# Masked cross attention with the mask of each key in the same matmul pass as the head's features

## The chip, the cores and the metric

The kernel runs on one core of a Trainium2 chip. The metric is the device time of one launch in microseconds (us). Five engines work in parallel, each through its own instructions in order: TensorE (PE, matmuls), VectorE (DVE), ScalarE (ACT), GpSimd (POOL) and SyncE (SP), which here issues nearly all DMA transfers. They wait for each other through semaphores.

## The reference, cut to what matters

A stream `x` of 4 batches of 512 tokens of 128 features passes four blocks of cross attention, each followed by a feed-forward block. The keys and values come from a context of 77 tokens. The fourth block is a decoder of four layers, each with causal self attention, masked cross attention and a feed-forward part. Masked cross attention is, for each head:

```python
scores = jnp.einsum('bhqd,bhkd->bhqk', q, k) / np.sqrt(DK).astype(jnp.float32)
scores = jnp.where(mask[:, None, :, :] == 0, jnp.float32(-1000000000.0), scores)
p_attn = jax.nn.softmax(scores, axis=-1)
x = jnp.einsum('bhqk,bhkd->bhqd', p_attn, v)
```

There are three masks: `l0` (all ones in these inputs) for block 0, `l1` (a padding mask or a mask by key) for block 1, `l3` (a window over segment numbers) for the four layers of block 3. Heads have 8 features, in block 1 there are 32 heads of 4.

## The kernel before

Cross attention is eight **units** of 16 heads (`UNITS`): 0 (mask `l0`), 1 and 2 (the two halves of block 1, mask `l1`), 3 (block 2, no mask), 4 to 7 (the layers, mask `l3`). A unit runs over 4 batches `b`; the heads lie in 4 groups `g` of 4 heads (`G`, `HG`). A head has 32 rows (`HR`): its features in a high part twice and a low part, and two rows for the negated maximum of each query, so that a product gives exact logits minus the maximum.

For each batch a unit does: normalise and project the queries (`stats`, `apply`, `turn`, `q_project`), project the context to keys and values (`kv_project`, `kv_cut`, `kv_spread`), cut the queries into parts (`q_cut`), transpose them (`q_turn`, into the buffers `q_g`), take scores with queries on the partitions for the maxima (`max`, lines 789 to 805 on PE, line 1311 on DVE), transpose again with the maxima in place (`q_full`), and then `logits` with keys on the partitions: eight tiles per batch, `logits(n, b, g, hp)`, each with two heads side by side. ACT takes the exponential (line 1791), and `values` multiplies by the values. In a masked unit a head's logits are **two** accumulating matmuls over 512 queries: the mask `bias_k` (77 keys, bf16) times the identity, then `kx` (the keys of the group, other heads' rows zero, 128 rows) times `q_g`.

`bias_q` (mask with queries on the partitions) is written by DVE: at the start for `l0`, in `masks1` (lines 1370 to 1381) for `l1`, in `masks3` for `l3`. `mask_turn` transposes it into `bias_k` on PE and ACT. SP's `masks1` (lines 638 to 651) does two things: it clears the tables `slots_in` and `slots_out` in DRAM from a blank row in `f2x`, which POOL zeroes as one of its first instructions, and it loads the raw `l1` masks, as soon as their buffer in `hid` is free.

The order of all work is written out by hand: `program_order` builds a list of steps, `interleaved` runs the phases of up to several batches (prepare, scores, attend, finish) beside each other, row by row, and every engine goes through that one list and does its share of each step. So the attend phase of a batch runs beside the scores phase of the next and the preparation of the one after. `need(...)` makes an engine wait for events, `made(...)` and `landed(...)` give them; `T.slot` and `T.freed` hand out buffers of a ring in order. PSUM has three `wide` buffers of two banks and two `acc` buffers, shared by all steps.

`f2x` holds the scales and the transposed values of the quantised feed-forward block (`quantise`, `turn("f2")`, `f2_matmul`), `f2_hid` its result.

Of the kernel before, what the change touches and what calls it, by code (L numbers as in the profile page):

```python
# [6 lines left out]
P = 128  # L7
# [8 lines left out]
MROW, KROW, QROW = 24, 26, 27  # L16
VSUM = 8
HIGH = -(1 << 12)
NEG = -float(2 ** 100)
E8 = 8  # L20
# [179 lines left out]

CLEARS = 9


def cross_steps(n):
    u = UNITS[n]

    def prepare(b):
# [9 lines left out]
        first = [[("apply", "u", n, b)], [], [], [("turn", "u", n, b)]] if u["first"] else []  # L217
        return s + beside(first, context_steps(n, b)) + query

    def scores(b):  # L220
        s = [[("q_turn", n, b, 0)]]
        for g in range(G):
            for half in range(2):
                s.append([("max", n, b, g, half)] + ([("q_full", n, b, g - 1)] if half and g else [])
                         + ([("q_turn", n, b, 1)] if g == 0 and half else []))
        return s

    def attend(b):
# [5 lines left out]
        tiles[7] += [("values", n, b, 2), ("o_turn", "u", n, b, 0)]  # L234
        return tiles + [[("o_norm", "u", n, b, 0)], [("values", n, b, 3)]]
# [116 lines left out]
def program_order():  # L352
# [17 lines left out]
    for l in range(NL):  # L370
        project, rotate, items = self_steps(l)
        if l == 0:
            items[5][0] = beside(items[5][0], in_rows(*[(3 * k, ("masks3", k)) for k in range(4)]))
            items[6][0] = beside(items[6][0], in_rows((5, ("mask_turn", "l3"))))
# [51 lines left out]
def build(nc, io):  # L426
# [4 lines left out]
    with ExitStack() as ctx:  # L431
# [30 lines left out]
        o_tok = bufs("o_tok", 2, lambda n: sb(f"o_tok{n}", [P, NI, D]))  # L462
        hid = bufs("hid", 2, lambda n: sb(f"hid{n}", [P, 4, S]))
        bias_q_raw = sb("bias_q", [P, NT * SK // 2])
        bias_k_raw = sb("bias_k", [P, B * S // 2])
        bias_q = bias_q_raw[:, :].bitcast(BF).rearrange("p (t k) -> p t k", t=NT)
        bias_k = bias_k_raw[:, :].bitcast(BF).rearrange("p (b s) -> p b s", b=B)
# [18 lines left out]
        f2_hid = bufs("f2_hid", 2, lambda n: sb(f"f2_hid{n}", [P, NI, D]))  # L486
        f2x = bufs("f2x", 2, lambda n: sb(f"f2x{n}", [P, 2 * NI + S // 2]))
# [3 lines left out]

        slots_in, slots_out = (nc.dram_tensor(name, (SLOTS + SPARE, D), F32) for name in ("slots_in", "slots_out"))
# [90 lines left out]
        def sync(e):  # L583
# [54 lines left out]
            def masks1():  # L638
                am_w, pm_w, *_ = raw_masks1()
                blank = f2x[0][:, 0:P]  # L640
# [10 lines left out]
                e.dma_start(pm_w, io["pad_mask"].partition_broadcast(P)).then_inc(*landed("load_masks1", ("masks1",)))  # L651

# [46 lines left out]
            do = dict(unit_end=unit_end, f0_down=f0_down, masks1=masks1, extras=extras, masks3=masks3, slots_in=slots_in_,  # L699
# [12 lines left out]
        def tensor(e):  # L712
# [94 lines left out]
            def logits(n, b, g, hp):  # L807
                masked, tile = UNITS[n]["masked"], ("logits", n, b, g, hp)
                s = wide[T.slot("wide", tile)]
# [1467 lines left out]
```

## Time and profile before

| | us |
|---|---|
| median of 3 runs | 2294.93 (2286.55 to 2299.99) |
| the profiled execution | 2294.56 |
| its span, first to last instruction | 2292.8 |

| engine | busy us | share of the span | instructions |
|---|---|---|---|
| PE | 1955.7 | 85% | 13195 |
| DVE | 1451.5 | 63% | 3533 |
| ACT | 1075.4 | 47% | 1517 |
| POOL | 634.3 | 28% | 865 |

Windows read below: 230.50 to 333.40 is unit 1, 1346.00 to 1372.90 one batch of unit 5, 1465.00 to 1695.20 the self attention of the third layer.

The mean granted TensorE clock is 0.907 of full speed (1.00 is 2.4 GHz, 0.50 is 1.2 GHz). Busy time of PE is modelled: matmuls are pipelined and overlap, so the start times tell more than the durations. PEld is the load of weights, beside PE. "idle before" in a row is the time for which the engine had nothing to do just before, with what released it. Masked logits run at 43 to 132 us (unit 0), 230 to 426 (1 and 2), 950 to 1038, 1320 to 1408, 1695 to 1784 and 2069 to 2158 (4 to 7).

### The profile page before, as it was taken

To read this page: it belongs to the slowest core of one execution; us is meant where nothing else is said; L and a number is where in the kernel's file an instruction comes from. 1 tells how busy PE (TensorE), PEld (TensorE's weight loads), DVE (VectorE), ACT (ScalarE), POOL (GpSimd) and SP (SyncE) were. 2 spreads that over 40 slices of the span, in tenths; PEclk is the share of its full clock that TensorE was granted. 3 is DMA by queue.
4 is the path that set the end of the run, shared out by engine and by line. 5 is a ranking of instruction groups with operands and counts; after the bars stand their busy time and mean duration, and the time that the engine had idled before them with its cause. 6 is when DMAs were issued, how large, how long until landed. Compare 5 with 4: busy or idle time off the path is not lost.

```text
span 2292.8 us, 34000 instructions
## 1 busy us (share of the span) xinstructions
PE 1955.7 (85%) x13195; PEld 1183.1 (52%) x13195; DVE 1451.5 (63%) x3533; ACT 1075.4 (47%) x1517; POOL 634.3 (28%) x865
## 2 busy tenths in 40 slices
PE   5977999585787798999799899898899988989977
PEld 4546666364544344555444565544455544456553
DVE  7545655653777777754666764567675467776468
ACT  2542555221453466553466455356545336545510
POOL 1111000423534353201444210345320144421020
PEclk9988999777786799999899899889889979989988
DMA  7001000121000000000000000000000000000000
GB/s 248 14 1 56 1 1 13 37 84 41 20 1 12 1 1 1 4 7 12 15 1 1 1 10 12 15 1 1 1 4 8 1 14 2 1 1 11 1 1 19
DMA packets 26929, 38.60 MB, mean 17 GB/s; under 512 B 5384, under 2 KB 20112, under 8 KB 26128
## 3 DMA queue, kind: packets, MB, share of 16 engines
q1 hardware_dynamic: 24720, 32.23, 4.3%
q0 software_dynamic: 2048, 4.20, 0.6%
q8 instruction: 104, 1.70, 0.3%
q14 instruction: 57, 0.47, 0.1%
HBM read 25.93 MB, written 10.49 MB: 16 GB/s over the span
## 4 chain that ended last, share of the span: by engine, by line
PE 46%; DVE 12%; ACT 5%; issue 5%; POOL 1%; DMA 0%; DVEq 0%; POOLq 0%; ACTq 0%
PE wide L717 33%; PE acc L717 13%; DVE maxima L1626 4%; ACT prob L1868 2%; DVE hid L1145 1%; DVE x L1687 1%; POOL rstd L1926 1%; DVE hid L1302 1%; ACT prob L1791 1%; DVE qkv L1594 1%; DVE hn L1223 1%; ACT hn L1756 1%; DVE hn L1225 0%; ACT q_g L1712 0%; DVE moments L1178 0%
## 5 line engine op out<-in xcount | busy, mean ns | idle before, releaser
L1626 DVE TENSOR_REDUCE maxima<-wide 128x2 f32<-128x512 f32 (+3 forms) x512 | 407.7, 820 | 182.9 <-PE wide L717 179.3
L1868 ACT ACTIVATE prob<-wide 128x768 f32<-128x768 f32 (+1 forms) x384 | 332.4, 881 | 157.9 <-PE wide L717 156.9
L1791 ACT ACTIVATE prob<-wide 77x1024 f32<-77x1024 f32 x256 | 260.4, 1018 | 148.8 <-PE wide L717 148.8
L717 PE MATMUL wide<-q_g 32*128 32x256 f32 (+3 forms) x2048 | 282.0, 417 | 41.1 <-ACT prob L1868 15.6
L1311 DVE TENSOR_REDUCE maxima<-wide 128x8 f32<-128x616 f32 x256 | 203.0, 796 | 169.4 <-PE wide L717 168.2
L2071 POOL TENSOR_SCALAR_AFFINE_SELECT prob<-prob 128x256 f32<-128x256 f32 (+1 forms) x384 | 185.7, 489 | 387.7 <-ACT prob L1868 383.7
L717 PEld LDWEIGHTS wide<-q_g 32*128 32x128 f32 x2048 | 147.2, 201 | 229.9 <-issue 114.8
L717 PE MATMUL wide<-q_g,kx 128*77 128x512 f32 x512 | 256.0, 572 | 7.7 <-DVE maxima L1311 5.4
L1926 POOL TENSOR_TENSOR rstd<-moments,cst 128x4 f32<-128x4 f32 x88 | 89.7, 1019 | 578.6 <-DVE moments L1199 296.3
L1712 ACT ACTIVATE q_g<-wide 128x1024 fp32r<-128x1024 f32 x128 | 131.2, 1025 | 209.1 <-PE wide L717 209.1
L1712 ACT ACTIVATE q_g<-acc 128x512 fp32r<-128x512 f32 x192 | 114.5, 596 | 186.6 <-PE acc L717 186.1
L717 PE MATMUL wide<-kx,q_g 128*128 128x312 f32 x512 | 181.3, 420 | 7.0 <-DVE maxima L1311 5.0
L717 PE MATMUL wide<-bias_k,ident_b 77*77 77x512 bf16 x448 | 172.4, 385 | 15.0 <-DVE vx L1246 8.7
L717 PE MATMUL acc<-cst,hid 128*128 128x128 f32 x768 | 123.2, 285 | 48.4 <-DVE hid L1302 48.4
L717 PE MATMUL wide<-cst,hid 128*128 128x128 f32 x768 | 122.9, 302 | 34.6 <-POOL A L2061 8.0
L717 PE MATMUL wide<-bias_q,ident_b 128*128 128x312 bf16 x448 | 135.8, 310 | 14.2 <-DVE vx L1246 10.2
L717 PE MATMUL acc<-prob,A 128*32 128x512 f32 (+3 forms) x1408 | 144.3, 486 | 0.0
L717 PE MATMUL acc<-prob,vx 77*32 77x512 f32 x1024 | 138.9, 615 | 0.0
L717 PE MATMUL wide<-causal_b,ident_b 128*128 128x128 bf16 (+1 forms) x768 | 134.4, 261 | 0.0
L717 PEld LDWEIGHTS wide<-cst,hid 128*128 128x128 f32 x768 | 96.0, 155 | 60.8 <-issue 24.2
L717 PE MATMUL wide<-hT,ffn_w 128*128 128x512 f32 x256 | 120.9, 597 | 3.9 <-DVE hid L1636 3.9
L717 PEld LDWEIGHTS acc<-cst,hid 128*128 128x128 f32 x768 | 93.7, 146 | 56.1 <-DVE hid L1302 43.0
(228 smaller groups left out, 3125.2 us busy)
## 6 DMA issues: line engine op xcount, KB each, us to landing
A<-in_w SPq DMA_DIRECT2D x2, 2048.0 KB, 12.4
unit_w<-in_unit_w SPq DMA_DIRECT2D x8, 448.0 KB, 3.4
ffn_w<-in_ffn_w SPq DMA_DIRECT2D x4, 768.0 KB, 4.4
slots_in<-f2x SPq DMA_DIRECT2D x1, 2560.0 KB, 23.6
prob<-slots_in SPq DMA_DIRECT2D x8, 320.0 KB, 3.1
slots_out<-A SPq DMA_DIRECT2D x8, 320.0 KB, 2.2
slots_out<-f2x SPq DMA_DIRECT2D x1, 2048.0 KB, 29.5
unit_w<-in_unit_rows SPq DMA_DIRECT2D x8, 192.0 KB, 4.1
```

Source lines behind the costliest of these rows:

```text
L717: return e.matmul(out, lhsT, rhs, start=start, stop=stop, is_transpose=turn)
L1145: return e.tensor_scalar(out.bitcast(I32), src.bitcast(I32), HIGH, None, ALU.bitwise_and)
L1223: i_op = e.tensor_scalar(dst[:, i, :], src[:, i, :], r[:, i:i + 1], None, ALU.mult)
L1302: return e.tensor_tensor(v[:, :, :, MROW + 1], top, v[:, :, :, MROW], ALU.subtract)
L1311: e.tensor_reduce(maxima[g % 2][:, 2 * half:2 * half + 2, :], v, AX.X, ALU.max, negate=True).then_inc(*made("max", ("free", tile)))
L1594: e.tensor_tensor(qkv[:, 2 * half:2 * half + 2, 0:2 * D], v[:, :, 0:2 * D], bias[:, :, 0:2 * D], ALU.add).then_inc(*made("qkv", ("qkv_adde ...
L1626: e.tensor_reduce(top[:, t, h], v[:, :, at0:at0 + P * t + P], AX.X, ALU.max, negate=True).then_inc(*made("max", *([("free", tile)] if t == ...
L1712: return e.activation(out, src, ACT.Copy, bias=0.0, scale=1.0)
L1791: e.activation(p[0:SC, :], s[0:SC, :], ACT.Exp, bias=0.0, scale=1.0).then_inc(*made("exp", pb, ("free", tile)))
L1868: e.activation(pv, sv, ACT.Exp, bias=0.0, scale=8 ** -0.5).then_inc(*made("exp", pb, ("free", tile)))
L1926: e.tensor_tensor(rstd[T.slot("rstd", held)][:, :], mo[:, 8 * NI:9 * NI], const("minus_half"), ALU.pow).then_inc(*made("rstd", held))
L2071: e.affine_select(out=v, in_=v, compare_op=ALU.is_ge, fill=0.0, base=0, pattern=[[0, many], [1, P]], channel_multiplier=-1).then_inc(*made ...
```

## The change

A masked head's logits become **one** matmul over 32 + 77 = 109 rows (`MASKED`): rows 0 to 31 are the head's own features, rows 32 to 108 one row for each key, with the identity in the keys' operand (`masked_k`) and the mask in the queries' operand (`masked_q`). A head's rows must be brought to partitions 0 to 31 for it, which SP does by DMA.

- New buffers: `masked_q`, three (`AHEAD`) of [128, 2, 512]; `masked_k`, two of [128, 2, 4, 79]; `alive`; `mask_rows`, the turned masks in DRAM. `bias_k` goes. To make room `f2_hid` moves into `A`, the transposed quantised values into one buffer within `bias_q`, and the blank row for the clears into `o_tok[0]`.
- `fetch(n, b, g, hp)` on SP copies two heads' queries from `q_g` into a `masked_q` buffer, 64 KB each, and for the first three tiles of a batch also the 77 mask rows, twice side by side (308 KB), from DRAM. It waits for the buffer (the logits three tiles before), `q_filled` and the mask. `fetch_keys(n, b, half)` copies the keys of 8 heads in 4 transfers. The fetch for tile k + 3 stands in the order behind the logits of tile k.
- `mask_turn` writes the turned mask into `masked_q` buffers; SP stores it to DRAM.
- Queries of which every key is masked are multiplied by zero (`find_alive` on DVE once per mask, a multiply of the projected queries on POOL once per batch of a masked unit); DVE's `q_cut` waits for that.
- POOL zeroes the blank row at its place in `masks1`, and SP's clears, and so its loads of the raw masks behind them, wait for that. `o_norm` of unit 1 waits for the clears. `masks3` and `mask_turn("l3")` stand four items later.

```diff
@@ scores(b), attend(b) in cross_steps
+        if b == 0:
+            for half in range(2):
+                s[4 + 4 * half] += fetch_keys(b, half)
+            for k in range(AHEAD):
+                s[6 + k] += fetch(b, k)
...
+        for k in range(2 * G):
+            tiles[k] += fetch(b + (k + AHEAD) // (2 * G), (k + AHEAD) % (2 * G))
+        tiles[4] += fetch_keys(b + 1, 0)
+        tiles[7] += fetch_keys(b + 1, 1)
@@ sync: masks1
-                blank = f2x[0][:, 0:P]
                 for w in need(("blank_rows",)):
                     e.wait_ge(*w)
                 e.dma_start(slots_in[0:SLOTS, :].rearrange("(p c) d -> p c d", p=P),
...
+            def mask_turn(name):
+                for w in need(("mask_turned", name)):
+                    e.wait_ge(*w)
+                for h in range(2):
+                    e.dma_start(mask_rows[name][:, 2 * h:2 * h + 2, :], masked_q[h][0:SC, :, :].bitcast(F32)).then_inc(
+                        *landed(f"store_mask_{name}", ("mask_k", name)))
+
+            def fetch(n, b, g, hp):
+                tile, name = ("masked_q", n, b, g, hp), UNITS[n]["masked"]
+                at = T.slot("masked_q", tile)
+                to, sem, q = masked_q[at], f"fetch{at}", q_g[T.slot("q_g", ("q_g", n, b, g // 2))][:, g % 2, :]
+                for w in need(T.freed("masked_q", tile), ("q_filled", n, b, g), ("mask_k", name)):
+                    e.wait_ge(*w)
+
+                if 2 * g + hp < AHEAD:
+                    e.dma_start(to[HR:MASKED, :, :].bitcast(F32), mask_rows[name][:, b, :].unsqueeze(1).broadcast_to([SC, 2, S])).then_inc(
+                        *landed(sem))
+                for ii in range(2):
+                    r = HR * (2 * hp + ii)
+                    e.dma_start(to[0:HR, ii, :].bitcast(F32), q[r:r + HR, :].bitcast(F32)).then_inc(*landed(sem, *([tile] if ii else [])))
+
+            def fetch_keys(n, b, half):
+                tile = ("masked_k", n, b, half)
+                at = T.slot("masked_k", tile)
+                for w in need(T.freed("masked_k", tile), ("kv", n, b), ("masked_ones",)):
+                    e.wait_ge(*w)
+                for i in range(HG):
+                    e.dma_start(masked_k[at][0:HR, :, i, :].bitcast(F32),
+                                kx[HR * i:HR * i + HR, i, 2 * half:2 * half + 2, SK * b:SK * b + SK].bitcast(F32)).then_inc(
+                        *landed(f"fetch_keys{at}", *([tile] if i == HG - 1 else [])))
@@ tensor: logits
-                for w in need(T.freed("wide", tile), ("mask_k", masked) if masked else None):
+                for w in need(T.freed("wide", tile), *((held, keys) if masked else (("q_filled", n, b, g),))):
...
                     if masked:
-                        mm(bank, ident_b[0:SC, 0:SC], bias_k[0:SC, b, :], stop=False)
-                    if ii == 0:
-                        for w in need(("q_filled", n, b, g)):
-                            e.wait_ge(*w)
-                    i_mm = mm(bank, kx[:, i, g, SK * b:SK * b + SC], q[:, :], start=not masked)
+                        i_mm = mm(bank, masked_k[T.slot("masked_k", keys)][0:MASKED, g % 2, i, 0:SC],
+                                  masked_q[T.slot("masked_q", held)][0:MASKED, ii, :])
+                    else:
+                        i_mm = mm(bank, kx[:, i, g, SK * b:SK * b + SC], q[:, :])
@@ vector
+            def find_alive(name):
+
+                after = {"l0": None, "l1": ("q_alive", 0, B - 1), "l3": ("q_alive", 2, B - 1)}[name]
+                for w in need(own(), after):
+                    e.wait_ge(*w)
+                e.tensor_reduce(alive[:, :], bias_q[:, :, 0:SC], AX.X, ALU.max).then_inc(*made("mask"))
+                for w in need(own()):
+                    e.wait_ge(*w)
+                e.tensor_scalar(alive[:, :], alive[:, :], 0.0, None, ALU.is_equal).then_inc(*made("mask", ("alive", name)))
@@ gpsimd
-            e.memset(f2x[0][:, 0:P], 0.0).then_inc(*made("begin", ("blank_rows",)))
...
+            def masks1():
+
+                for w in need(own()):
+                    e.wait_ge(*w)
+                e.memset(blank, 0.0).then_inc(*made("clear", ("blank_rows",)))
+
+            def q_project(n, b):
+                if not UNITS[n]["masked"]:
+                    return
+                dh = UNITS[n]["dh"]
+                v = qkv[:, :, 0:16 * dh]
+                for w in need(("q_added", n, b), ("alive", UNITS[n]["masked"])):
+                    e.wait_ge(*w)
+                e.tensor_tensor(v, v, alive[:, NI * b:NI * b + NI].unsqueeze(2).broadcast_to([P, NI, 16 * dh]),
+                                ALU.mult).then_inc(*made("q", ("q_alive", n, b)))
```

## Rows read from the trace of the kernel before

**Rows 1.** Page, parts 1 and 4: busy time, and the chain by engine.

```profile
PE 1955.7 (85%) x13195; PEld 1183.1 (52%) x13195; DVE 1451.5 (63%) x3533; ACT 1075.4 (47%) x1517; POOL 634.3 (28%) x865
...
PE 46%; DVE 12%; ACT 5%; issue 5%; POOL 1%; DMA 0%; DVEq 0%; POOLq 0%; ACTq 0%
```

**Rows 2.** Windows: length, busy PE, PEld, DVE, ACT, POOL; clock, DMA share, GB/s.

```profile
230.50:333.40 102.90, 98.45 (x670) 63.63 (x668) 63.38 (x155) 57.59 (x70) 6.46 (x10) 1.00 0.00 1
1346.00:1372.90 26.90, 24.90 (x172) 16.25 (x171) 17.70 (x46) 14.50 (x18) 2.61 (x3) 1.00 0.00 1
1465.00:1695.20 230.20, 204.46 (x1597) 109.82 (x1597) 161.27 (x296) 124.99 (x173) 91.98 (x141) 0.87 0.01 4
```

**Rows 3.** Groups of instructions by form: the mask matmuls (busy us, mean ns).

```profile
L717 PE MATMUL wide<-bias_k,ident_b 77*77 77x512 bf16 x448 | 172.4, 385 | 15.0 <-DVE vx L1246 8.7 <-ACT prob L1791 4.3 <-DVE qkv L1467 0.9
```

**Rows 4.** Timeline of PE in unit 4 (start us, us): one logits tile.

```profile
989.86 0.38 PE L717 MATMUL wide<-bias_k,ident_b 77*77 77x512 bf16 x1
...
990.31 0.38 PE L717 MATMUL wide<-bias_k,ident_b 77*77 77x512 bf16 x1
...
990.76 1.05 PE L717 MATMUL wide<-unit_w,hT 128*128 128x128 f32 x8
```

**Rows 5.** Timeline of PE in unit 3, no mask: one logits tile.

```profile
629.29 0.71 PE L717 MATMUL wide<-q_g,kx 128*77 128x512 f32 x2
629.84 1.05 PE L717 MATMUL wide<-unit_w,hT 128*128 128x128 f32 x8
```

**Rows 6.** Timeline of PE in unit 4: a batch's second logits tile.

```profile
980.87 0.41 PE L717 MATMUL wide<-bias_k,ident_b 77*77 77x512 bf16 x1 [1.47 <-DVE vx L1246]
```

**Rows 7.** Windows: unit 0's first batches.

```profile
40.00:50.00 10.00, 7.01 (x50) 5.67 (x51) 8.37 (x27) 3.76 (x5) 1.57 (x2) 1.00 0.50 145
```

**Rows 8.** Timeline of PE, last batch of unit 7: tiles 3, 4 and 7.

```profile
2149.90 0.41 PE L717 MATMUL wide<-bias_k,ident_b 77*77 77x512 bf16 x1 [0.47 <-ACT prob L1791]
...
2151.91 0.41 PE L717 MATMUL wide<-bias_k,ident_b 77*77 77x512 bf16 x1
...
2157.17 0.38 PE L717 MATMUL wide<-bias_k,ident_b 77*77 77x512 bf16 x1
```

**Rows 9.** Timeline of SP's DMA issues: x, the clears, the raw masks.

```profile
5.86 5.84 SPq L618 DMA_DIRECT2D x<-in_x  x4
...
15.68 0.61 SPq L643 DMA_DIRECT2D slots_in<-f2x  x1
16.34 20.22 SPq L646 DMA_DIRECT2D slots_out<-f2x  x1
98.97 0.38 SPq L650 DMA_DIRECT2D hid<-in_attn_mask  x1
```

**Rows 10.** DMA issues by line: KB each, median us from issue to landing.

```profile
slots_in<-f2x SPq DMA_DIRECT2D x1, 2560.0 KB, 23.6
...
slots_out<-A SPq DMA_DIRECT2D x8, 320.0 KB, 2.2
slots_out<-f2x SPq DMA_DIRECT2D x1, 2048.0 KB, 29.5
...
hid<-in_pad_mask SPq DMA_DIRECT2D x1, 40.0 KB, 3.7
```

**Rows 11.** Timelines of DVE and of POOL around masks1.

```profile
136.35 1.65 DVE L1376 TENSOR_TENSOR hid<-hid 128x308 f32<-128x308 uint8 x4
...
136.45 1.26 POOL L1926 TENSOR_TENSOR rstd<-moments,cst 128x4 f32<-128x4 f32 x1 [11.84 <-DVE moments L1202]
```

**Rows 12.** Groups by form on POOL and DVE: multiply and reduction of similar size.

```profile
L1964 POOL TENSOR_TENSOR x<-x,o_tok 128x512 f32<-128x512 f32 x4 | 5.1, 1268 | 20.1 <-DVE o_tok L1328 11.2 <-issue 4.6 <-DVE hn L1225 4.4
...
L1571 DVE TENSOR_TENSOR hid<-cst,hid 128x1232 f32<-128x1232 f32 x1 | 1.4, 1435 | 0.0
```

**Rows 13.** Timeline of DVE in unit 4: q_project's add, q_cut's first step.

```profile
991.92 0.69 DVE L1277 TENSOR_TENSOR qkv<-wide,unit_w 128x512 f32<-128x512 f32 x1 [1.05 <-PE wide L717]
...
994.25 0.43 DVE L1145 TENSOR_SCALAR hid<-qkv 128x512 int32<-128x512 int32 x1
```

More of the change, by code:

```diff
@@ L197, in context_steps @@
     return [[("kv_project", n, b)], [("kv_cut", n, b)], [("kv_spread", n, b, 0)], [("kv_spread", n, b, 2)]]
+AHEAD = 3
 CLEARS = 9
@@ L217, in prepare @@
         first = [[("apply", "u", n, b)], [], [], [("turn", "u", n, b)]] if u["first"] else []
+        if (n, b) == (0, 0):
+            query = [[("alive", "l0")]] + query
         return s + beside(first, context_steps(n, b)) + query
@@ L225, in scores, with fetch, fetch_keys @@
                          + ([("q_turn", n, b, 1)] if g == 0 and half else []))
-        return s
+        if b == 0:
[3 more added lines that the diff above has]
+                s[6 + k] += fetch(b, k)
+        return s
+    def fetch(b, pair):
+        return [("fetch", n, b, pair // 2, pair % 2)] if u["masked"] and b < B else []
+    def fetch_keys(b, half):
+        return [("fetch_keys", n, b, half)] if u["masked"] and b < B else []
     def attend(b):
@@ L372, in program_order @@
         if l == 0:
-            items[5][0] = beside(items[5][0], in_rows(*[(3 * k, ("masks3", k)) for k in range(4)]))
-            items[6][0] = beside(items[6][0], in_rows((5, ("mask_turn", "l3"))))
+            items[9][0] = beside(items[9][0], in_rows(*[(3 * k, ("masks3", k)) for k in range(4)]))
+            items[10][0] = beside(items[10][0], in_rows((5, ("mask_turn", "l3"))))
             every.append([[]])
@@ L697, in m_store @@
                     *landed(f"out{b}", ("stored", b)))
-            do = dict(unit_end=unit_end, f0_down=f0_down, masks1=masks1, extras=extras, masks3=masks3, slots_in=slots_in_,
+            do = dict(mask_turn=mask_turn, fetch=fetch, fetch_keys=fetch_keys, unit_end=unit_end, f0_down=f0_down, masks1=masks1, extras=extras, masks3=masks3, slots_in=slots_in_,
                       f1_out=f1_out,
@@ L1284, in q_cut @@
                 src = qkv[:, :, 0:D].rearrange("p t (h r) -> p t h r", r=dh)[:, :, 0:16, :]
-                for w in need(own(), T.freed("hid", ("qt", n, b))):
+                for w in need(own(), T.freed("hid", ("qt", n, b)), ("q_alive", n, b) if UNITS[n]["masked"] else None):
                     e.wait_ge(*w)
@@ L1325, in o_norm @@
                 out = ot[:, :, 2 * HG * g * dh:(2 * HG * g + 2 * HG) * dh].rearrange("p t (i r) -> p t i r", i=2 * HG)
-                for w in need(own(), T.freed("o_tok", held)):
+                for w in need(own(), T.freed("o_tok", held), ("slots_blank",) if (kind, k) == ("u", 1) else None):
                     e.wait_ge(*w)
@@ L1546, in f2_matmul @@
             def f2_matmul(b):
-                s, xs = wide[T.slot("wide", ("f2_matmul", b))], f2x[T.slot("f2x", ("f2", b))]
+                s, xs = wide[T.slot("wide", ("f2_matmul", b))], f2_scale[T.slot("f2_scale", ("f2", b))]
                 hv = f2_hid[T.slot("f2_hid", ("f2_hid", b))][:, :, :]
-                for w in need(own(), ("f2_matmul", b), T.freed("f2_hid", ("f2_hid", b))):
+                for w in need(own(), ("f2_matmul", b), T.freed("f2_hid", ("f2_hid", b)), ("f1_down", E8 - 1)):
                     e.wait_ge(*w)
@@ L1737, in turn @@
                 elif kind == "f2":
-                    for w in need(tile):
+                    for w in need(tile, T.freed("f2_q", ("f2_q", b))):
                         e.wait_ge(*w)
-                    i_op = copy(f2x[T.slot("f2x", ("f2", b))][:, 2 * NI:].bitcast(BF), s)
+                    i_op = copy(f2_q[T.slot("f2_q", ("f2_q", b))], s)
                 else:
```

46 lines of the change are left out of this document (31 added, 15 removed).

## The prediction

> **What bounds the kernel now.** I read the busy shares and the chain first. TensorE (PE) is busy 85% of the span and carries 46% of the chain that ended last, DVE 12%, ACT 5%, DMA nothing [rows 1]. An average over stages says little, so next the windows by stage. A masked unit of cross attention (there are seven: 0, 1, 2 and 4 to 7, some 90 to 100 us each) runs PE 98.45 of 102.90 us at clock 1.00; inside one, a batch takes 26.90 us with PE 24.90, DVE 17.70, ACT 14.50 [rows 2]. PE is the bound there, and what leaves PE there can shorten the time. The self-attention stage (PE 204.46 of 230.20 us, clock 0.87) isn't touched but for small steps.
>
> **What goes from PE.** Seven units of 4 batches of 8 tiles make 224 logits tiles, and each loses its two mask matmuls: 448, mean 385 ns [rows 3]. That mean isn't the price, since matmuls overlap. Starts are: in a masked tile head to head is 990.31 - 989.86 = 0.45 us, and the next work (the projection with hT) starts 0.90 us after the tile [rows 4]. In unit 3, which has no mask, the same tile of two matmuls, in front of the same projection and at clock 1.00, takes 629.84 - 629.29 = 0.55 us [rows 5]. The changed tile has that form: same columns, other operands. So 0.35 us go per tile, 224 x 0.35 = 78.4 us. The upper bound is a whole 0.45 (the cost halved exactly): 101 us. I take 0.35, because its row is the form itself. The Trainium skill (TensorE: Matmul & The Clock Gate, section "Back-to-back issue gap") gives an isolated matmul of N columns N/2.4 + 2.5 ns at full clock, 216 ns for 512. That rule would make it 448 x 0.216 = 97 us, an estimate from the page; the row says less, probably since the weights' load is part of what remains.
>
> **How much of that arrives.** Not every tile stands behind PE work. (a) After the first tile of a batch PE waits 1.47 us for DVE's chain of the context keys and values (L1246) [rows 6]; DVE is the later one there, and PE merely arrives sooner: 28 tiles x 0.35 = 9.8 us lost. (b) From 40 to 50 us PE works 7.01 of 10 us and DVE 8.37 [rows 7]: unit 0's first two batches are DVE's, 14 more tiles, 4.9 us lost. (c) The last batch of a unit has no other batch's maxima beside it. There PE already waits 0.47 us for ACT's exponential [rows 8], and a tile's ACT work is longer than its matmuls; I count half for 7 x 7 tiles, 8.6 us lost. Realised: 78.4 - 9.8 - 4.9 - 8.6 = **55.1 us**. Bounds: 25 (a further half lost in the other tiles, if dependencies bind as in c) and 78.
>
> **What the fetches cost.** Per batch SP now issues 8 x 2 query copies, 3 mask copies (only for the first AHEAD = 3 tiles) and 2 x 4 key copies: 27. An issue takes 0.38 us on an idle queue and 0.61 in the loaded one; the dearest row is 5.84 us for four, 1.46 each, behind the first loads [rows 9]. At 0.47 (0.38 and the step to the next) that is 12.7 us of a batch's 26.9. The copy for tile k+3 waits until tile k frees its buffer. The trace has no SBUF to SBUF copy; the nearest is 320 KB to DRAM, 2.2 us from issue to landing, and 3.7 for the pad mask [rows 10]. Tile k's end to landing: 0.1 + 0.47 + 2.2 to 3.7 = 2.8 to 4.3 us. Room: the tightest pair, tiles 4 and 7 of a last batch, is 2157.17 - 2151.91 = 5.26 us start to start [rows 8]; less the tile (0.55) and three savings (1.05) leaves 3.7. Elsewhere it is some 8 us. So fetches are hidden, except at tails: 0 to 10 us, I take 3. Were the room gone, each tile would pay the missing part (rival C). PE's wait gets nothing new queued behind it but the next tiles; the queries' wait it replaces (q_filled) is earlier in the same chain.
>
> **What goes wrong at masks1.** This is the largest cost. Before, SP issued the two clears of the slot tables at 15.68 and 16.34, before any wait, and the two loads of raw masks at 98.97 [rows 9], when the queue was empty. DVE took them at 136.35 with no wait [rows 11]. Now the blank row is in o_tok, which unit 0 uses, and Pool blanks it at masks1, behind the rstd that starts at 136.45 and takes 1.26 [rows 11]: some 138.0. SP then issues both clears and *behind them, in the same queue,* the mask loads, on which DVE waits in masks1 with all later work of the stage behind it. The clears are 2560 and 2048 KB. They landed at 15.68 + 23.6 = 39.3 and 16.34 + 29.5 = 45.8 [rows 9, 10], so the second alone took 6.5 us, and both need 4608/2048 x 6.5 = 14.6. Masks land at 138.0 + 0.6 + 14.6 + about 2.5 = 155.7; DVE stands for 155.7 - 136.35 = **19.4 us**. Nothing covers it: PE's mask_turn and ACT's copies wait for DVE, and two hidden tiles more is all PE can do. Bounds 0 (loads overtake) and 23. Cold PE afterwards: 2 us.
>
> **The smaller steps.** alive: a reduction over 1232 elements, nearest row 1435 ns [rows 12], with its compare 1.6 us. At l1 it is on the stalled path, +1.6; at l3 DVE has gaps, +0.8; at l0, with Pool's first multiply (nearest 1268 ns [rows 12]) in the first batch's path, +1.7 since DVE waited there anyway. Pool's multiply later: DVE adds the projection at 991.92 and cuts at 994.25, with a maximum between [rows 13]; from the add's end there are 1.6 us, and 1.27 + 0.1 fits, so 0. In the first batches of units 4 to 7 Pool has the causal selects of self attention in order before it, and DVE waits behind them: 4 x 1 = 4 us (0 to 12). Clears leave the start, where nothing waited for them: 0. Moving masks3, f2_hid into A, one buffer for f2_q, and o_norm's wait for the clears (done by then): 0; if the clears were late, unit 1's first o_norm would wait.
>
> **Sum.** -55.1 + 3 + 19.4 + 2 + 1.6 + 0.8 + 1.7 + 4 = -22.6 us. Against the profiled execution's 2294.56 (span 2292.8, and 1.8 around it; the median of the runs is 2294.93) that is **2272.0 us**.
>
> **The rivals.**
> A. *The clears hide.* The mask loads land beside them or DVE's stall finds cover. For it: transfers run on many engines. Against: SP itself stood 20.22 us in the second clear [rows 9], so the queue is full and the loads are issued late. It gives 2272 - 19 = 2253.
> B. *DVE or ACT becomes the bound in masked units.* A batch has DVE 17.70 and ACT 14.50 beside PE, which falls to 22.1 [rows 2], and DVE's work lies in one half of the batch. The wait of 1.47 us grows and others appear. Realised 25 instead of 55: 2302, slower. It decides from 55.1 - 22.6 = 32.5 us realised downwards. Against: only 4 of 90 us are idle today.
> C. *SP or the fetch is late.* 27 issues are a bound once one costs over (26.9 - 7 x 0.35)/27 = 0.91 us; 1.46 has been seen, though in a full queue [rows 9]. At 1.0 us a batch takes 27.0 instead of 24.4, 28 x 2.6 = 73 us more: 2345.
> D. *The clock falls.* Self attention, PE 89% busy, is granted 0.87 [rows 2]; masked units would come to some 90%. At 0.95 there, PE's 7 x 77 us become 27 longer: 2299. Against: 40 to 50 us, PE 70% busy, has 1.00 [rows 7]. The Trainium skill (same page, "What's actually happening") says the gate follows how busy PE has been recently, which is this rival's rule; the row at 70% speaks against its biting here.
> E. *The pass doesn't get cheaper* (fp32r weights of 109 rows cost what the bf16 pass saved): only costs stay, 2294.6 + 32.5 = 2327.
>
> **Chances.** Forecast 0.48, A 0.14, B 0.15, C 0.11, D 0.08, E 0.04. The range that leaves about 2 in 10 out runs from A's 2253 down a little to B's 2302 up a little: 2248 to 2308. About 0.5% (11.5 us) can be told from no change. Faster (under 2283.5): most of the forecast's case and A, 0.58; within 0.5% (2283.5 to 2306.4): edges of the forecast, half of B and D, 0.20; slower 0.22.
>
> **What would show it.** Logits tiles of two matmuls 0.55 us apart; masked windows some 8 us shorter each at clock 1.00; DVE's masks1 op with an idle of some 19 us before it, released by a DMA; PE's idle before logits tiles released by DMA near zero but at tails; SP issues near 0.43. Wrong it would be if PE waits on fetches in the middle of units, if the wait on L1246 takes more than its 0.35 per batch, or if the stall at masks1 is missing.

## The result and the profile after

The changed kernel takes 2278.51 us (median of 16 runs, 2269.04 to 2293.78) against 2294.22 us for the kernel before in its 16 runs beside it: ratio 0.9934, with a 95% interval from 0.9912 to 0.9957. That is 15 us faster, with 10 to 20 in the interval. The forecast was 2272.0. The profiled execution took 2272.35 us (span 2270.6) against 2294.56 before.

Busy time and the chain from the page of the changed kernel answer to [rows 1]; the last three lines are from its view of PE's waits (us in total, times, longest us):

```profile
PE 1889.2 (83%) x12747; PEld 1137.4 (50%) x12747; DVE 1451.9 (64%) x3539; ACT 1065.9 (47%) x1517; POOL 662.9 (29%) x895
...
PE 43%; DVE 11%; ACT 5%; issue 5%; POOL 2%; SPq 1%; DMA 1%; DVEq 0%; POOLq 0%
...
PE wide L777 <- DVE bias_q L1452: 21.5, 1, 21.5
PE wide L777 <- ACT prob L1942: 16.2, 50, 0.4
PE wide L777 <- DMA masked_q<-q_g: 14.3, 11, 2.6
```

448 matmuls are gone (13195 to 12747), and DVE has as much to do as before. Two waits are new: 21.5 us once, for DVE's work on the raw masks, and 14.3 us for query copies (the row of ACT's prob was there before, with 15.6). The tile itself, from the timeline of PE in unit 5 (start, duration, line, output and inputs):

```profile
1395.50 0.60 PE L777 MATMUL acc<-cst,hid 128*128 128x128 f32 x4
1395.86 0.71 PE L777 MATMUL wide<-masked_q,masked_k 109*77 109x512 f32 x2
1396.41 0.31 PE L777 MATMUL wide<-bias_q,ident_b 128*128 128x312 bf16 x1
```

From the tile's start to the next work are 0.55 us, as [rows 5] said; it was 0.90 [rows 4]. Next the windows, from the start of a masked unit's first logits matmul to the start of its last: unit 0, units 1 and 2 together, units 4, 5, 6 and 7; the last row is the stage between units 0 and 1 (first feed-forward and masks1). Columns: length, busy us of PE, PEld, DVE, ACT and POOL, granted clock, DMA share, GB/s.

```profile
47.88:125.53 77.65, 69.92 (x442) 40.94 (x442) 49.64 (x133) 48.40 (x61) 13.13 (x13) 0.96 0.39 100
247.71:428.02 180.31, 164.84 (x1098) 104.28 (x1097) 114.77 (x306) 104.85 (x134) 24.89 (x32) 0.96 0.35 97
967.94:1049.66 81.72, 76.33 (x513) 47.93 (x512) 48.69 (x120) 50.47 (x65) 10.27 (x12) 0.94 0.38 99
1333.93:1413.89 79.96, 74.05 (x514) 45.87 (x512) 48.75 (x120) 50.46 (x65) 10.28 (x12) 0.98 0.37 98
1693.40:1772.29 78.89, 72.69 (x513) 44.80 (x512) 48.72 (x120) 50.46 (x65) 10.27 (x12) 1.00 0.38 98
2051.74:2135.70 83.96, 78.22 (x514) 47.42 (x512) 48.96 (x120) 50.63 (x65) 10.29 (x12) 0.92 0.37 92
125.53:247.71 122.18, 70.26 (x472) 58.96 (x471) 54.79 (x175) 33.47 (x89) 18.45 (x20) 0.78 0.29 86
```

The six windows add up to 582.5 us; the same cuts through the profile of before give 639.4 (89.0, 194.5 and four of 89.0). So 57 us came out of the masked units, and the rest of the kernel gave 35 of them back: the stage with masks1 grew from 98.8 to 122.2, the start up to the first logits tile from 42.7 to 47.9, the part from unit 2 to unit 4 from 524.9 to 539.9 (13 of these 15 us go with a lower clock), while the three self attentions after it fell by 9. The clock column is the second thing to see: masked units stood at 1.00 but for unit 0 (0.96), and now only one of the windows does.

That makes an account worth keeping for every run: time x (1 - mean granted clock), called the *lost time* here, and what is left. It is bookkeeping and no model (a wait at half clock counts half), but it is repeatable: where a kernel was timed twice, what is left agrees within 5 us, and for the kernel before, timed on three chips, within 6.

### The profile page after: what moved, and what is told of

Same layout as the page of the kernel before. It is cut to its first block, busy times and chain, and to the rows that moved or that the text cites. A ratio compares the mean times of both kernels' runs of the same rounds, so it can differ in the third digit from the quotient of the medians.

```text
span 2270.6 us, 34236 instructions
## 1 busy us (share of the span) xinstructions
PE 1889.2 (83%) x12747; PEld 1137.4 (50%) x12747; DVE 1451.9 (64%) x3539; ACT 1065.9 (47%) x1517; POOL 662.9 (29%) x895
## 4 chain that ended last, share of the span: by engine, by line
PE 43%; DVE 11%; ACT 5%; issue 5%; POOL 2%; SPq 1%; DMA 1%; DVEq 0%; POOLq 0%
PE wide L777 31%; PE acc L777 13%; DVE maxima L1700 4%; ACT prob L1942 2%; DVE hid L1207 1%; DMA masked_q<-q_g 1%; DVE x L1761 1%; POOL rstd L1999 1%; SPq L701 1%; ACT prob L1865 1%; DVE qkv L1668 1%; DVE hn L1295 1%; DVE hn L1297 0%; ACT hn L1830 0%; ACT q_g L1786 0%
## 5 line engine op out<-in xcount | busy, mean ns | idle before, releaser
L777 PE MATMUL wide<-masked_q,masked_k 109*77 109x512 f32 x448 | 158.2, 438 | 33.7 <-DMA masked_q<-q_g 14.3
L777 PE MATMUL wide<-cst,hn 128*128 128x128 f32 x320 | 59.9, 319 | 69.3 <-DVE hn L1297 50.3
## 6 DMA issues: line engine op xcount, KB each, us to landing
masked_k<-kx SPq DMA_DIRECT2D x224, 19.5 KB, 2.4
A<-in_w SPq DMA_DIRECT2D x2, 2048.0 KB, 12.7
```

The costliest lines, as they stand in the source:

```text
L777: return e.matmul(out, lhsT, rhs, start=start, stop=stop, is_transpose=turn)
```

## The experiments

Every run below was timed in five rounds beside the kernel before. Medians, with the ratio to before of the same chip:

```
kernel                     us     ratio   interval         clock   lost   left
before                   2282.0                            0.911   203    2079
changed                  2278.5   0.9934  0.9912-0.9957    0.887   257    2021
before, clears late      2307.0   1.0104  1.0078-1.0130    0.906   217    2090
before, no pass          2223.2   0.9742  0.9718-0.9766    0.896   231    1992
changed, loads first     2250.8   0.9864  0.9829-0.9899    0.890   248    2003
  the same again         2250.3   0.9860  0.9824-0.9896    0.891   245    2005
changed, clears at start 2251.7   0.9860  0.9833-0.9886    0.891   245    2006
loads first, no multiply 2243.7   0.9777  0.9752-0.9801    0.893   241    2003
  the same again         2235.6   0.9793  0.9765-0.9820    0.894   237    1999
  multiply twice         2277.4   0.9975  0.9954-0.9996    0.886   261    2017
  no fetch               2249.7   0.9803  0.9784-0.9822    0.892   243    2007
  keys on Pool           2258.9   0.9860  0.9840-0.9881    0.886   258    2001
  the same again         2242.7   0.9815  0.9784-0.9846    0.894   237    2006
  keys twice             2324.9   1.0127  1.0097-1.0157    0.883   272    2053
```

The row of before is that of the first set, in which the next four were run. Chips differ by about 0.5% (the kernel before took 2294.2 us beside the changed kernel and 2282.0, 2293.3 and 2282.7 beside the three sets), so ratios are compared, not microseconds; differences in lost time and left below some 5 us say nothing. The windows below come from one profiled execution of each kernel, and the profile of before (2294.56 us) is 12 us longer than its median in the first set.

### The moved clears alone, on the kernel before

On Pool, the blanking at the start no longer releases the clears; a second one, a step of masks1, does:

```
- e.memset(f2x[0][:, 0:P], 0.0).then_inc(*made("begin", ("blank_rows",)))
+ e.memset(f2x[0][:, 0:P], 0.0).then_inc(*made("begin"))
...
+ def masks1():
+     for w in need(own()):
+         e.wait_ge(*w)
+     e.memset(f2x[0][:, 0:P], 0.0).then_inc(*made("clear", ("blank_rows",)))
```

> The kernel before, with one part of the change alone: Pool blanks the zero row at masks1 instead of at the start, so both clears of the slot tables are issued there, in front of the two raw mask loads on SP's queue. Theory (the stall at masks1 is what the moved clears cost, and it lies wholly on the path): DVE's masks1 operation has an idle of 20 to 22 us before it, as in the changed kernel (21.8), and the time is 2294.2 + 20 = 2314 (2309 to 2322; ratio 1.009). Rival 1 (the stall finds cover later, since the stage afterwards has slack): within 5 us of before. Rival 2 (the stall also starts a stretch at half clock that costs beyond it; the changed kernel's stage there grew by 23.5 us, with 24 us more of it at half clock, and the MoE stage by 15): 2325 to 2335.

DVE's group in this run (busy, mean ns, idle before it and its releaser), and the stage with masks1:

```profile
L1376 DVE TENSOR_TENSOR hid<-hid 128x308 f32<-128x308 uint8 x4 | 1.6, 474 | 23.1 <-DMA hid<-in_pad_mask 23.1
133.09:255.02 121.93, 71.24 (x474) 60.19 (x473) 52.37 (x174) 33.55 (x89) 17.21 (x18) 0.79 0.24 71
```

DVE stands 23.1 us, and the stage grows by as much (98.8 to 121.9). The time rises by 0.0104 x 2282 = 24 us (18 to 30). The rival of a cover later falls, and so does that of a further cost behind the stall (31 to 41 us).

### The pass alone, on the kernel before

```
-   if masked:
-       mm(bank, ident_b[0:SC, 0:SC], bias_k[0:SC, b, :], stop=False)
...
```

The lines left out here let the product that follows start a fresh sum, here and in the tiles of the maxima, so that the mask has no effect anywhere.

> The kernel before without the mask's pass in the 224 logits tiles (448 matmuls of 128x512 left out) and with nothing in its place, so no fetches. Left out of the computation: the mask. So that the exponents stay finite, the mask is also overwritten in the tiles of the maxima: there each mask matmul still runs, but the next one starts a fresh sum. Theory (224 x 0.35 = 78.4 us go, of which 55 arrive at the end, the rest standing behind DVE's context chain, DVE's part of unit 0 and ACT's end of a unit): 2294.2 - 55 = 2239 (2232 to 2248; ratio 0.976). Rival (the fetches took part of it in the changed kernel: PE stood 14 us behind query copies there): all masked units together 65 to 70 us shorter, 2226. Rival (the clock falls when the pass goes, in other stages too): 2250 to 2260, with masked units at 1.00 and self attention longer than before.

59 us (53 to 64) went, 4 more than the theory. The masked windows add up to 571.0 us, 68 less than in the profile of before, as the first rival said (65 to 70); but its time of 2226 stood for 68 us less, and that is outside the interval. Window and time differ since the profile of before was 12 us longer than the median here. Three of the windows, units 0, 4 and 6:

```profile
43.77:124.93 81.16, 71.51 (x445) 42.61 (x443) 50.25 (x137) 48.78 (x62) 11.03 (x11) 0.92 0.06 18
927.24:1005.82 78.58, 73.68 (x513) 46.11 (x512) 48.48 (x120) 50.43 (x65) 8.23 (x10) 0.98 0.03 8
1646.61:1723.73 77.12, 72.22 (x513) 44.76 (x512) 48.48 (x120) 50.25 (x65) 8.23 (x10) 1.00 0.03 8
```

Without any fetch the clock falls in masked units too: lost time in them is 17.0 us, where it was 3.4. So the last rival was right that the clock falls, and wrong on the place and the size: it had the masked units at 1.00 and self attention longer, where three self attentions took 845.1 us against 851.8. The pass is worth 68 us of masked span, and 82 with the lost time taken off (0.37 us for each of 224 tiles), and part of that comes back as a lower clock, in every run without the pass.

### The mask loads ahead of the clears, and the clears at the start

In SP's masks1, the first of the two; the second (not shown) moves the blanking, the wait and both clears to the start, ahead of all steps, and lets unit 0's first output wait for the clears:

```
+ for w in need(T.freed("hid", ("raw", "l1"))):
+     e.wait_ge(*w)
+ e.dma_start(am_w, io["attn_mask"].rearrange("(i p) k -> p i k", p=P)).then_inc(*landed("load_masks1"))
+ e.dma_start(pm_w, io["pad_mask"].partition_broadcast(P)).then_inc(*landed("load_masks1", ("masks1",)))
  for w in need(("blank_rows",)):
      e.wait_ge(*w)
...
- for w in need(T.freed("hid", ("raw", "l1"))):
-     e.wait_ge(*w)
- e.dma_start(am_w, io["attn_mask"].rearrange("(i p) k -> p i k", p=P)).then_inc(*landed("load_masks1"))
- e.dma_start(pm_w, io["pad_mask"].partition_broadcast(P)).then_inc(*landed("load_masks1", ("masks1",)))
```

> The changed kernel, with the two raw mask loads issued ahead of the two clears in SP's masks1; nothing else. Theory (DVE waits for the loads only since they are queued behind the clears): the idle before DVE's masks1 operation falls from 21.8 to 3 to 6 us (a load of 3.7 us to landing, and DVE reaches masks1 as SP does), time 2278.5 - 17 = 2261 (2255 to 2266; ratio to before 0.986). Rival (PE stands there anyway, behind DVE's other work or at half clock): no change, 2278. Rival (the clears, now later, delay the first slots-dependent work: unit 1's first output operation waits for them): 2270.

> The changed kernel, with the zero row in the same buffer but blanked at the start and the clears issued there, as in the kernel before; unit 0's first output operation waits for them instead of unit 1's. Theory: DVE's wait at masks1 is gone altogether (0 to 1 us), time 2278.5 - 21.8 = 2257 (2251 to 2262; ratio 0.984), some 3 us better than with the loads first. Rival (the clears of 26 us on the queue at the start delay the first keys and queries, issued from 38.7 us): the first logits of unit 0 come later than 47.9 us and 2260 to 2265. Rival (stall not on the path): 2278.

SP's queue in the changed kernel, then with the loads first:

```profile
131.38 0.60 SPq L672 DMA_DIRECT2D slots_in<-o_tok  x1
132.03 7.32 SPq L675 DMA_DIRECT2D slots_out<-o_tok  x1
139.40 7.28 SPq L679 DMA_DIRECT2D hid<-in_attn_mask  x1
146.73 1.32 SPq L680 DMA_DIRECT2D hid<-in_pad_mask  x1
```

```profile
121.51 0.59 SPq L672 DMA_DIRECT2D hid<-in_attn_mask  x1
122.15 0.52 SPq L673 DMA_DIRECT2D hid<-in_pad_mask  x1
131.21 0.61 SPq L676 DMA_DIRECT2D slots_in<-o_tok  x1
131.87 7.27 SPq L679 DMA_DIRECT2D slots_out<-o_tok  x1
...
L1448 DVE TENSOR_TENSOR hid<-hid 128x308 f32<-128x308 uint8 x4 | 1.6, 472 | 0.0
```

The loads no longer wait for Pool's blanking either, so they go out 10 us before the clears and DVE finds them there: its idle is 0.0, less than the 3 to 6 us expected. The stage is back at 101.3 us, and the ratio falls from 0.9934 to 0.9864, 16 us (6 to 26). Clears at the start reach the same 0.9860 by another way: DVE's wait is gone too, but the first logits tile comes at 53.7 us instead of 46.9, as that run's rival said. Both versions beat both kernels (2251 us).

### Without fetches

No copy is issued at all, and the logits are read as in the kernel before; as in the run without the pass, the mask has no effect (that part isn't shown):

```
-     for w in need(T.freed("wide", tile), *((held, keys) if masked else (("q_filled", n, b, g),))):
+     for w in need(T.freed("wide", tile), ("q_filled", n, b, g)):
...
-         if masked:
-             i_mm = mm(bank, masked_k[T.slot("masked_k", keys)][0:MASKED, g % 2, i, 0:SC],
-                       masked_q[T.slot("masked_q", held)][0:MASKED, ii, :])
-         else:
-             i_mm = mm(bank, kx[:, i, g, SK * b:SK * b + SC], q[:, :])
+         i_mm = mm(bank, kx[:, i, g, SK * b:SK * b + SC], q[:, :])
```

> Stands on the run with the mask loads first (ratio 0.9864). The logits are read from the same tiles as in the kernel before, so no query, mask or key is copied; the multiplies, the searches for keyless queries and the moved clears stay. Left out of the computation: the mask (in the tiles of the maxima its matmuls run and are then overwritten). Theory (PE stands 14 us behind the copies at the ends of units, and ACT and the buffers of wide some us more): 0.9864 - 0.0070 = 0.979 (0.977 to 0.981). Rival (the copies cost what the prediction gave them, 3 us): 0.985. Rival (they are the whole difference to the kernel before without the pass): 0.974.

0.9803, in the theory's range: the fetches cost (0.9862 - 0.9803) x 2293 = 14 us (6 to 21). Masked windows add up to 570.4 us against 589.0 and 584.8 in the two runs of its base, 14 to 19 us. Nearly all of that is lost time: 16.8 us against 33.1 and 28.2, while the part that is left is 553.6 against 555.9 and 556.7. Unit 4 shows it, in the base (second run) and without fetches:

```profile
937.25:1023.53 86.28, 80.85 (x513) 49.90 (x512) 48.96 (x120) 50.88 (x65) 10.27 (x12) 0.89 0.35 91
```

```profile
948.18:1026.81 78.63, 73.71 (x514) 46.10 (x512) 48.72 (x120) 50.42 (x65) 10.27 (x12) 0.98 0.03 8
```

The mask copies (308 KB each, three in a batch) were never left out alone, so how the cost is shared between query, mask and key copies is open.

### The key copies: on Pool, and twice on SP

Keys on Pool moves fetch_keys word for word from SP's functions to Pool's. Keys twice puts this ahead of the four copies on SP:

```
+ for i in range(HG):
+     e.dma_start(extra_keys[2 * (B * n + b) + half, i], kx[HR * i:HR * i + HR, i, 2 * half:2 * half + 2, SK * b:SK * b + SK].bitcast(F32)).then_inc(
+         *landed(f"fetch_keys{at}"))
```

> Stands on the run with the mask loads first (ratio 0.9864). SP issues every key copy twice, the first time to a place in DRAM that nobody reads: 35 issues in a batch instead of 27. Theory (an issue costs SP some 0.6 us, so a batch's copies take 21 us instead of 16, more than the 19 us that a batch takes): SP is the bound in the masked units, 28 x 2 to 28 x 4 us more, ratio 1.01 to 1.04, with PE's waits for query copies in the middle of units too. Rival (SP is behind only at the ends of units): 28 x 0.5 = 14 us more, 0.9925. Rival (the issue isn't what PE waits for): no change.

> Stands on the run with the mask loads first (ratio 0.9864). The key copies, 8 of the 27 issues of a batch, are issued by Pool instead of SP, at the same places of the order. Theory (SP is behind at the end of a unit since it issues without a gap there: 19 issues instead of 27 give it 5 us more): PE's waits for query copies fall from 14 us to under 4, ratio 0.9864 - 0.004 = 0.982. Rival (Pool's issues take over 1 us each and stand in front of its rstd and multiplies: 56 x 4 us of Pool): 0.988 to 0.995, with PE waiting for hn and qkv longer. Rival (waits are the copies' landing, not their issue): no change.

> The key copies on Pool, again, beside its base. The first time PE's waits for query copies fell from 14.2 to 2.2 us and the masked units' spans from 582.9 to 576.3 us together, but the medians were the same (0.9860 against 0.9864, on different chips and at a clock of 0.886 against 0.890). Theory (6 us are gained, and the clock hid them): 3 to 9 us under its base. Rival (what is late next takes all of it): within 2 us.

PE's waits for query copies in the run with double keys, and in the first one with keys on Pool, where two more rows changed (in the base the waits for ACT's oT, the transposed output of attention, and DVE's o_tok, the output before it, are 8.0 and 8.7 us):

```profile
PE wide L781 <- DMA masked_q<-q_g: 60.6, 39, 3.1
```

```profile
PE wide L767 <- ACT oT L1776: 12.9, 24, 1.2
PE wide L767 <- DVE o_tok L1390: 12.3, 9, 5.5
PE wide L767 <- DMA masked_q<-q_g: 2.2, 5, 0.6
```

Eight more issues in a batch cost 0.0265 x 2293 = 61 us, and PE's wait grows by 46, in 39 places instead of 9: SP is then the bound. (They also move 8 x 19.5 KB more in a batch; no run separates that.) The changed kernel is close to that edge. Its SP in unit 5, at the passage from the third batch to the last, and PE's first late tile:

```profile
1393.27 2.57 SPq L709 DMA_DIRECT2D masked_k<-kx  x4
1395.93 0.48 SPq L697 DMA_DIRECT2D masked_q<-mask_l  x1
1396.45 1.19 SPq L701 DMA_DIRECT2D masked_q<-q_g  x2
...
1401.19 2.57 SPq L709 DMA_DIRECT2D masked_k<-kx  x4
1403.80 7.75 SPq L701 DMA_DIRECT2D masked_q<-q_g  x10
...
1403.75 0.66 PE L777 MATMUL wide<-masked_q,masked_k 109*77 109x512 f32 x2 [1.93 <-DMA masked_q<-q_g]
```

From 1393.27 to 1403.77 SP issues 17 copies without a gap, 0.62 us each: four keys, three times a mask and two queries, four keys. Tile 1 of the last batch is the one that waits: its second query copy is the later of the two issued between 1398.26 and 1399.40, from about 1398.8, and PE is let go at 1403.75, 4.9 us later. With keys on Pool (some 2.2 us for four there, as the trace has it) PE's wait falls from 14.2 to 2.2 us, and from 12.7 to 3.1 in the second pair. The time didn't follow in the first run (0.9860 against 0.9864) and did in the second (0.9815 against 0.9860 on the same chip, 10 us, 0 to 21), where the theory said 3 to 9; masked windows are 582.2 and 584.4 us against 589.0 and 584.8 (the 576.3 and 582.9 of the expectation end at the row that merges the last two tiles, about 1 us early in each unit). Of 12 us of wait in the first pair, 8.5 came back as waits for ACT's oT and DVE's o_tok, which are late next. Whether 0 or 10 us are left of it, these runs don't settle. The Trainium skill (DMA: Bandwidth & Descriptors, section "Issuing engines are not separate DMA queues") says that another issuing engine saves only the sequencer's time to initiate the DMA, which is usually small beside the DMA itself; here that time is what PE waited for, and the row shows it go.

### The multiply by the keyless flag: left out, and twice

Left out: the body of find_alive on DVE, Pool's q_project and the wait for it in DVE's q_cut. Twice, on Pool in q_project, ahead of the one that is there:

```
+ e.tensor_tensor(v, v, alive[:, NI * b:NI * b + NI].unsqueeze(2).broadcast_to([P, NI, 16 * dh]),
+                 ALU.mult).then_inc(*made("q"))
+ for w in need(own()):
+     e.wait_ge(*w)
```

> Stands on the run with the mask loads first (2250.8 us against 2282.0, ratio 0.9864), not on the changed kernel itself. Left out: the three searches for keyless queries and Pool's 28 multiplies of the projected queries by that flag; queries are cut as they come. Theory (start +1.7, l1 1.6, l3 0.8, self attention 4 us: 8 us): 0.9864 - 0.0036 = 0.983. Since the start itself grew by 5.2 us instead of 1.7, 10 to 12 us and 0.982 are as likely. Rival (Pool's step stands in the queries' path of every batch, 28 x 1.0 us, so most of the 27 us between this kernel and the kernel before without the pass): 0.975. Rival (DVE had slack everywhere): 0.986.

> The run with the mask loads first again, as the base beside which the next three are read on the same chip. It should give 0.9864 again within its interval (0.983 to 0.990), and by the mean granted clock of its runs 1.7 us less for each 0.001 of clock, as the runs of one kernel did so far (slope some -1700 us for 1.0 of clock within each kernel).

> Without the searches for keyless queries and Pool's multiplies, again, beside its base. The first time it gave 0.9777, 20 us under its base by the medians, while the stages of the two profiles differ by 3 us at equal clock, and the base was timed on another chip. Theory (they cost 3 to 8 us, the rest was chance): 0.983 to 0.986. Rival (they cost 20 us, spread thinly): 0.978.

> On the same base, with Pool's multiply made twice in every masked batch (the flag is 0 or 1, so the second changes nothing): 28 more operations of 1.04 us, which DVE's cut of the queries waits for. Theory (DVE and PE have other work there): 0 to +6 us, ratio 0.986 to 0.989. Rival (each stands on the path, as 20 us for 28 of them says): +20 to +29 us, 0.995 to 0.999.

The base came out the same (0.9860). Leaving searches and multiplies out gains 20 us in the first run and 15 (5 to 26) in the second, on the base's own chip; a second multiply costs 0.0115 x 2283 = 26 us (16 to 37) for 29 us of Pool's work. My theories of "3 to 8, the rest is chance" and of 0 to 6 us for the second multiply fall, and both rivals hold. DVE's waits for the multiply, in the base and with two:

```profile
DVE hid L1207 <- POOL qkv L2022: 6.7, 13, 1.2
```

```profile
DVE hid L1207 <- POOL qkv L2026: 24.5, 21, 2.3
```

One multiply is covered in 15 of 28 batches and costs DVE 6.7 us; two are covered in 7. In the stages, the doubling adds 3.2 us at the start (46.8 to 49.9), 4.3 in the stage with masks1, 5.1 from unit 3 to unit 4 and 9 in the masked units. The three later self-attention stages grew from 281.8 to 285.8 us each, all of it lost time (68.7 to 81.2 us together). Whether the multiply lowers the clock there or the profiled execution had it so by chance stays open; the median clock of its 12 runs is lower too (0.886 against 0.891).

For the removal the profiles don't show such a place. Without searches and multiplies the start is 1.2 to 1.9 us shorter (45.7 and 44.9) and the stage with masks1 about 1 us, but the masked units aren't shorter (586.9 and 591.4 us). In the table the part that is left falls by 6 us in the same set (2005 to 1999), near the 8.1 of the prediction's terms, and the lost time by 8 (245 to 237). So that these steps cost 15 to 20 us is measured; that all of it is a wait for the multiply is not shown.

## Why the prediction was right, and where it wasn't

The forecast of 2272 stands 6.5 us from the median and in range, but two errors cancel: the gain was larger than summed, and so were the costs, the largest of them one that the sum didn't have. That the number came so close is in part luck.

**What goes from PE: right in mechanism, too small in size.** The tile is 0.55 us as read from unit 3. The "224 x 0.35 = 78.4 us" was called a sum before losses, and 55.1 were to arrive; alone, the pass brings 68 us of masked span and 59 us of time. In unit 6, at 1.00 in both profiles, the window fell by 11.8 us, and 32 x 0.35 is 11.2: nothing was lost there to (a) and (c). In unit 0, where (b) took 4.9 us off, it fell by 7.8 us, and by 11.2 with the lost time taken off. The waits that these counted did grow in the changed kernel, but little: PE's wait for vx from 33.2 us over the whole kernel to 39.8, that for maxima from 18.4 to 24.6, that for ACT's exponential fell from 14.6 to 13.1. The prediction took half of every tile of a last batch away on one wait of 0.47 us [rows 8]. The Trainium skill's rule, which the prediction worked out (TensorE: Matmul & The Clock Gate, section "Back-to-back issue gap"), gave 97 us; with the lost time taken off these runs show 82, nearer to the row's 78. The section itself says that this figure, for an isolated matmul, counts too much at large N in a stream of them.

**The clock: a term that the sum didn't have.** It was rival D at 0.08, held off with "40 to 50 us, PE 70% busy, has 1.00" [rows 7]. One stretch at 1.00 in the first 50 us was no evidence for units much later. Unit 7 of the changed kernel shows a fall; timeline, then windows:

```profile
2117.98 0.69 PE L777 MATMUL wide<-masked_q,masked_k 109*77 109x512 f32 x2
2120.53 0.66 PE L777 MATMUL wide<-masked_q,masked_k 109*77 109x512 f32 x2 [1.85 <-DMA masked_q<-q_g]
...
2116.00:2119.00 3.00, 2.67 (x19) 1.09 (x17) 2.17 (x7) 0.89 (x2) 0.00 (x0) 1.00 0.68 199
2119.00:2122.00 3.00, 1.47 (x10) 1.15 (x10) 1.66 (x12) 1.99 (x3) 1.01 (x1) 1.00 0.62 161
2122.00:2125.00 3.00, 1.97 (x8) 1.16 (x7) 1.35 (x5) 1.83 (x4) 0.00 (x0) 0.66 0.33 81
2125.00:2128.00 3.00, 3.00 (x11) 0.60 (x12) 0.00 (x0) 1.51 (x2) 0.00 (x0) 0.50 0.32 77
```

PE works 1.47 and 1.97 of 3 us, then goes on at 0.50 (the level of 1.2 GHz) although it is busy again. Lost time in the masked units is 3.4 us before, 24.2 after and 17.0 without pass and fetch. Over the whole kernel it rises from 213 us in the profiled execution of before (2294.56 x 0.093) to 250 in that of after (2272.35 x 0.11) and to 257 in the median run; the part that is left falls from 2081 to 2021. So 60 us were gained at the old clock, and 37 to 44 given back. In the two profiles 21 of these are in the masked units, 14 in the stage with the stall and 3 in all the rest. That the lower share of PE's work in the masked units is the cause is shown as far as this: it goes with every kernel without the pass, with fetches and without, and with neither of the two that keep it (3.4 and 5.1 us). The fetches go with more of it: 33.1 and 28.2 us in the two profiles with the loads first, 16.8 with the fetches out. No run held the clock, so this is a pattern over fourteen profiles and not a proof.

**The fetches: mechanism named, size four to five times too small (3, measured 14).** The step that failed is the room of "the tightest pair, tiles 4 and 7", with 0.47 us an issue and 2.8 to 4.3 us to landing. It asked whether one copy lands in its gap. What binds is SP's backlog at the passage of two batches, 17 issues at 0.62 us, and a copy in that row takes 4.9 us from issue to release; in a last batch PE catches up with it, at tile 1. Rival C's arithmetic (27 issues against a batch) had the right form with a wrong batch: it took 24.4 us, where the windows give four batches in 78 to 84 us. At 20 us a batch the edge is 0.74 us an issue, or 32 issues at 0.62; double keys (35, 21.7 us) are past it. The issues that were to be "near 0.43" took 0.62. How the price is paid the sum couldn't have either: of the 14 to 19 us that the fetches cost in the masked units, 2 to 3 are left with the lost time taken off, the size of the forecast's 3, and the rest goes with a lower clock.

**masks1: right.** "19.4 us" was 21.8 in the changed kernel and 23.1 alone:

```profile
151.77 1.65 DVE L1448 TENSOR_TENSOR hid<-hid 128x308 f32<-128x308 uint8 x4 [21.82 <-DMA hid<-in_pad_mask]
```

The path was as told: blanking, clears, then the loads behind them in SP's queue. Its times were not: the first clear went out at 131.38 instead of 138, 1.4 us after DVE had come, and the masks landed 20.4 us behind it instead of 17.7. PE's own wait of 21.5 us says that nothing covered it. Rival A falls. The "2 us" for cold PE came from no row, and nothing like it is seen: with the clears late alone the stage grew by 23.1 us for a stall of 23.1.

**The smaller steps: the multiply was costed wrong.** "From the add's end there are 1.6 us, and 1.27 + 0.1 fits, so 0" was read off one batch [rows 13]; over 28 it fits in 15. With searches it costs 15 to 20 us by removal where the terms gave 8.1 (1.6, 0.8, 1.7 and 4). At the start the term of 1.7 was about right: the search and its compare take 1.6 before DVE's add, DVE then waits 1.23 more for Pool, and removing them gives 1.2 to 1.9 us back. But the first logits tile came 5.1 us later than before, and no run separates the other 3.

```profile
22.03 1.44 DVE L1237 TENSOR_REDUCE alive<-bias_q 128x16 f32<-128x1232 bf16 x1
...
25.63 0.76 DVE L1207 TENSOR_SCALAR hid<-qkv 128x512 int32<-128x512 int32 x1 [1.23 <-POOL qkv L2022]
```

**The sum, measured.** Pass -59, fetches +14, clears +24, searches and multiplies +15 to +20: -1 to -6, where the kernel shows -15 (-20 to -10). Each term carries 5 to 11 us either way, so the parts and the whole are compatible. They needn't be additive either, since the clock falls differently in each kernel. Rival B (DVE or ACT becomes the bound) is seen only as what is late next, when fetches no longer are; E is out, since the new tile takes 0.55 us where the old one took 0.90.

## What to carry to other kernels

When a step is moved on a queue, look at what comes behind it there: two large writes put in front of two small loads cost this change more (24 us alone) than it gained in the end (15), and the loads issued ahead of them gave 16 us back. Count a DMA issue as work of the engine that issues it, and add up the issues of the busiest stretch and not of one tile. Where PE is the bound and gets less to do, put a price on the granted clock: here part of what left came back as a slower rest, and the runs' time minus lost time (within 5 us between repeats) tells a kernel's own change from the clock's.

## What was unexpected of the hardware

**One stage, two clocks.** The stage from unit 5's last two logits tiles to unit 6's first has the same PE work in these two kernels (keys on Pool, then no fetch):

```profile
1386.51:1664.23 277.72, 247.44 (x1857) 138.32 (x1856) 186.25 (x378) 143.16 (x207) 113.36 (x165) 0.94 0.04 12
```

```profile
1388.88:1675.30 286.42, 256.64 (x1857) 142.33 (x1855) 188.66 (x378) 144.10 (x207) 108.80 (x157) 0.90 0.02 6
```

8.7 us, for 10 us more of lost time (the clocks are 0.939 and 0.905). Between runs of one kernel, 0.001 of mean clock goes with about 1.5 us, over all 132 runs that have a clock; the six runs with the loads first, spread over 22 to 23 us, go with it. What made the clock differ is open.

**A short load pays for long writes.** The issue of a mask load takes 0.59 us on a free queue and 7.28 us behind the two clears: the issuing engine itself stood, and the pad mask's issue behind it began only at 146.73.
